# Two extra full-height products behind every first attention pass of the first unit of heads

## What is computed

```
x = x + attention_a(layernorm(x))       # 16 heads of 8, rotary, no mask            "stage a"
x = x + local_stack(layernorm(x))       # 6 layers, windows of 32, feed-forward     "stage b"
x = x + attention_c(layernorm(x))       # 16 heads of 8, rotary, causal mask        "stage c"
x = x + attention_and_experts(x)        # 4 heads, 8 experts                        "stage d"

# attention_a, attention_c, per head:
scores = q @ k.T / sqrt(8)              # attention_c: only keys up to the query
out = softmax(scores) @ v
```

## Time and profile before

| | |
|---|---|
| time, median of 3 runs | 5325.54 us (5321.98, 5325.54, 5348.38) |
| span of the profiled execution, first to last instruction | 5311.3 us |
| lowest run above that span | 10.7 us |
| TensorE matmul (PE) busy | 4908.3 us, 92% |
| TensorE weight load (PEld) busy | 2986.5 us, 56% |
| VectorE (DVE) busy | 4424.3 us, 83% |
| ScalarE (ACT) busy | 3628.7 us, 68% |
| GpSimd (POOL) busy | 2893.4 us, 54% |
| mean granted TensorE clock | 0.959 of 2.4 GHz |

### The profile page before, as it was taken

The page is one execution under the profiler, slowest core; times in us unless marked ns, Lnnn a source line. Parts: engine busy times, 40 slices in busy tenths (PEclk is TensorE's granted clock), DMA queues, the critical chain, the costliest instruction groups (busy, mean ns, idle before and its releaser), DMA issues. The chain is left out here.

```text
span 5311.3 us, 143059 instructions
## 1 busy us (share of the span) xinstructions
PE 4908.3 (92%) x59480; PEld 2986.5 (56%) x59480; DVE 4424.3 (83%) x9261; ACT 3628.7 (68%) x6488; POOL 2893.4 (54%) x3441
## 2 busy tenths in 40 slices
PE   6999997999999999999999999999997999968978
PEld 2333333666666666666666666666664555544445
DVE  7998995989999899999899889999985777677665
ACT  2888885777777777777777777777772777745622
POOL 2121003878777777787778777877761111024634
PEclk6999998999999999999999999999996999988989
DMA  0000101000000000000000000000000000000000
GB/s 23 1 1 1 32 5 39 10 10 14 26 10 10 14 26 10 10 17 26 10 10 14 26 10 10 14 10 10 8 4 25 2 2 2 2 15 1 1 1 17
DMA packets 51737, 63.29 MB, mean 12 GB/s; under 512 B 12820, under 2 KB 41258, under 8 KB 50322
## 3 DMA queue, kind: packets, MB, share of 16 engines
q1 hardware_dynamic: 51090, 54.14, 3.4%
HBM read 25.17 MB, written 4.19 MB: 6 GB/s over the span
## 5 line engine op out<-in xcount | busy, mean ns | idle before, releaser
L1488 POOL TENSOR_TENSOR x<-x,b_norm 128x512 f32<-128x512 f32 x768 | 784.5, 1042 | 350.9 <-DVE b_norm L1353 350.8
L1143 PE MATMUL psum<-b_w_vo,b_mixed 128*128 128x128 f32 x6144 | 830.2, 278 | 2.9 <-ACT b_mixed L1242 1.5
L1143 PEld LDWEIGHTS psum<-b_w_vo,b_mixed 128*128 128x128 f32 x6144 | 753.4, 192 | 68.0 <-issue 51.1
L652 DVE TENSOR_REDUCE a_top<-psum 128x1 f32<-128x512 f32 x1024 | 637.5, 682 | 77.9 <-PE psum L471 75.5
L1479 POOL TENSOR_TENSOR x<-x,b_cross 128x256 f32<-128x256 f32 x768 | 559.6, 729 | 186.4 <-DVE b_cross L1337 185.5
L583 ACT ACTIVATE a_prob<-psum 128x512 f32<-128x512 f32 x1024 | 557.1, 606 | 117.9 <-PE psum L487 108.5
L1212 ACT ACTIVATE b_square<-psum 128x512 f32<-128x512 f32 x768 | 465.5, 606 | 162.8 <-DVE b_norm L1345 144.3
L1345 DVE TENSOR_REDUCE b_norm<-b_square 128x8 f32<-128x512 f32 x768 | 514.1, 673 | 61.3 <-ACT b_square L1212 60.8
L1242 ACT COPY b_mixed<-psum 128x512 f32<-128x512 f32 x768 | 409.1, 588 | 223.4 <-PE psum L1128 223.4
L1481 POOL TENSOR_TENSOR x<-x,b_cross 128x256 f32<-128x256 f32 x768 | 559.5, 728 | 0.0
L1333 DVE TENSOR_TENSOR x<-psum,b_table 128x512 f32<-128x512 f32 x768 | 520.5, 678 | 23.1 <-ACT b_square L1212 23.1
(11 more groups left out here) (321 smaller groups left out, 10471.6 us busy)
## 6 DMA issues: line engine op xcount, KB each, us to landing
b_prev<-b_xs_x SPq DMA_DIRECT2D x24, 384.0 KB, 3.5
b_shifted_x<-y SPq DMA_DIRECT2D x24, 224.0 KB, 2.6
b_shifted_f<-y SPq DMA_DIRECT2D x48, 112.0 KB, 2.1
ab<-in_L_ffn_Wqkv SPq DMA_DIRECT2D x3, 1024.0 KB, 7.0
ab<-in_L_ffn_Wqkv SPq DMA_DIRECT2D x6, 512.0 KB, 7.2
ab<-in_L_ffn_Wo SPq DMA_DIRECT2D x6, 512.0 KB, 8.7
b_w_qk<-in_L_ffn_Wqkv SPq DMA_DIRECT2D x3, 1024.0 KB, 7.2
b_prev<-b_xs_x SPq DMA_DIRECT2D x24, 112.0 KB, 3.4
```

The lines of the kernel that those rows point to most:

```text
L652: e.tensor_reduce(top2[i % 2][:, t, c, head:head + 1], banks[n][:, 0:wide], AX.X, ALU.max).then_inc(emptied[n], 1)
L1143: made = e.matmul(banks[n][:, 0:D], mixed[:, h, :], w_vo[l % 2][:, h, :], start=h == 0, stop=h == 2 * PAIRS - 1)
L1488: e.tensor_tensor(rh, rh, bcast(norm[i % 2][:, 1, HPC * c:HPC * (c + 1)], 2, LDIM), ALU.mult).then_inc(sem["scaled"], 1)
```

## The change

In the branch of TensorE's stream that writes a first pass, two more matmuls follow it when the unit is the stage's first (`i == 0`). They multiply all 128 rows of the same query and key columns (so all four heads at once, full height and width of the array), as wide as the pass itself, into bank 7. Bank 7 holds nothing at that time: the values of unit 0 come later and start it anew, so what these products write is never read. They carry no semaphore. `mha_stage` is built for stage a and for stage c, so both have them: 2 x 64 products in a, 2 x 48 in c.

```diff
@@ -471,6 +471,10 @@
                     e.matmul(banks[n][:, 0:wide], q1[i % 2][part, P * t:P * (t + 1)], kt[i % 3][part, BANK * c:hi],
                              start=not corner, stop=True, skip_group_check=corner,
                              tile_position=(ROWS * head, 0)).then_inc(filled[n], 1)
+                    if i == 0:
+                        for _ in range(2):
+                            e.matmul(banks[7][:, 0:wide], q1[0][:, P * t:P * (t + 1)], kt[0][:, BANK * c:hi],
+                                     start=True, stop=True, skip_group_check=True)
                 if kind == "second":
                     c, k, g = step[2:]
                     lo = max(0, k * P - c * BANK) if causal else 0
```

## The result

The changed kernel takes 5415.6 us as the median of 4 runs (5388.63 to 5420.94), the kernel before 5323.76 us (4 runs, 5313.28 to 5348.38). The ratio is 1.0161, with a 95% interval of 1.0144 to 1.0178: 1.6% slower. The profiled execution spans 5415.3 us and took 5416.56 us, so only 1.3 us lie around a span.

What follows compares the result with a forecast made beforehand. VectorE was taken to bound stage a's start until 72.3 us, then TensorE at 1.2 GHz; with pairs, TensorE throughout. +13 - 4 + 42 = +51 us on 5325.5 gave 5376.5 us; own range 5365 to 5400, whole range 5341 to 5440.

Steps and rivals of the forecast that it cites:

- B: Rival: the clock falls in stage a too, say at VectorE's norms, and stays down; +66 there, 5439 us; chance 0.10.
- D: Rival: the added products take twice the columns or more; at twice, about 5435 us; chance 0.04.
- The bound: Unit 0 of stage a: with the pairs TensorE becomes the bound all through, as VectorE needs only 0.61 us a pass.
- The price of a pass and its pair: First pass plus two products on TensorE: 1.02 us at full clock, 1.76 at half, changes of height included.
- The upper bound given beside it: Price of a pair if each product took 1,024 columns: 1.28 us more at half clock, half that at full.
- E: Rival: changes of height cost next to nothing, only columns count; sum +9, 5335 us; chance 0.03.
- Which clock? At 46 us it is full: Stage a, unit 0: clock full on entry and kept with the pairs; 71.1 us against 58.2, +13.
- Unit 1 of stage a: Entered at full clock instead of half: first 19 passes take 13.3 us in place of 17.0, -4; then the clock falls.
- Stage c: Unit 0: narrow pairs lose the clock, 84.3 us against 37.3, +47, less 5 for the opening: +42; unit 1: 0.
- C: Rival: in stage c the clock returns after the transposes for about half; 42 shrinks to about 22, 5355 us; chance 0.19.
- Rival A: Clock holds at 1.00 through unit 0 and the start of unit 1 in both stages; +7, 5332 us; chance 0.11.
- The time around the span: Whole kernel: the span of 5311.3 us lies 10.7 below the lowest of three runs, 14.2 below their median.

Runs made afterwards that it cites:

- the entry filled: Changed kernel plus dense float32 products ahead of unit 0: 21 (stage c 15) before turn_k, 3 before turn_q1, gaps closed; 5391.74 us, ratio 1.0138.
- The control: Kernel before plus the same dense float32 products ahead of unit 0, without pairs behind the passes; 5320.96 us, ratio 1.0005.

## Why the prediction was right, and where not

The direction and the range held (5341 to 5440), but 5415.6 us lie outside the forecast's own 5365 to 5400: the loss was 92 us where 51 were forecast. The range held it because it was drawn wide enough for B and D.

- **The bound.** Right. TensorE is the bound in both units 0, without a gap, and VectorE waits for it.
- **The price of a pass and its pair.** Right in kind, a little low. 1.76 us at half clock were forecast, 1.87 measured; 1.02 and 1.09 at full. The pass's 0.72 was exact; the pair took 1.15 in place of 1.04, four transposes being a good but not perfect stand-in. An fp32r product goes through once: a pair takes 1.15 us at half clock, and twice the columns alone would be 1.71, so D falls. (The upper bound given beside it is miscounted: 1,024 columns a product add 0.85 us a pair at half clock, not 1.28. D itself has the right sum.) E falls too: one product in place of two left 75 of 92 us, and seven tenths of the loss in the units 0, where columns alone would leave half.
- **The failed step: "Which clock? At 46 us it is full".** I took the clock on entry from one execution of the kernel before, where nothing in unit 0 depended much on it. With the pairs it decides: in stage a they kept the clock that they found, for 72 us at full and 92 at half. In the profiled execution it was half, and stage a cost +52.7 in place of +9. With the entry filled it cost 12.6, within the forecast's ends of +5 and +13, and in five of ten executions with stage a alone the whole loss was 3 to 10 us. The term was right where its condition held, which by the two groups is about every other time. This was rival B but for its ways: B had the clock fall at a norm and stay down (+66), while it never was up at the entry and came back at 138.9 us, behind transposes and a projection between pairs. With the condition met the sum is still low: 69 us with the entry filled, in place of 51.
- **Unit 1 of stage a.** Right: 19 passes in 11.9 us at full clock where 13.3 were forecast, and the clock fell again before the values, for 17.0 us.
- **Stage c.** The mechanism was right, the size low: +42 forecast, +50.5 in unit 0 of the profiled execution, +52 with stage c alone. Unit 0 took 87.8 us against the 84.3 worked out, the pair's price again; the 5 us taken off for a clock that comes back had no ground, it stayed at 0.50 to the end. C didn't happen.
- **Rival A and the rule behind it.** No. TensorE was busy 84.40 of 84.40 us in stage c at a clock of 0.50, and the 3.4 us before, at 1.00, had no gap either. The Trainium skill ("TensorE: Matmul & The Clock Gate", section Why this matters for your kernels) asks for no idle gaps; here that was not enough. The row that the prediction set against A doesn't show this: the clock fell at 48.7 us, and in the 3.4 us before, at 1.00, TensorE was busy only 2.13 us, which left idle time as a cause. The products of 32 rows show it (busy 3.35 of 3.40 us, then 0.50), and stage c of the changed kernel does. In these traces the full clock lasted longest where full-height products of 512 columns stood behind the passes; narrow pairs, products of 32 rows and bare passes lost it. Which property of the work decides isn't shown.
- **The time around the span** was taken as 10.7 us and is 1.3; the other 9 are the spread between executions. It didn't enter the sum, which was put on the median.

What stays open: of the 70.7 us between the spans of the filled entry and of the kernel before, about 13 are in stage a and about 47 in the start of stage c, counted by the starts of VectorE's same instructions in both. About 4 lie between the two stages and about 6 around the end of stage c. There the clock stood at 0.50 for 27.3 us in a row (4662.5 to 4689.8), in the kernel before for 6.8 (4605.5 to 4612.3). The control, entry without pairs, has the same 27.3 us (4595.4 to 4622.7), so it comes without the pairs too. The clock falls and rises there at other places in each execution, and no run says why.

## What to carry to other kernels

A filler that is to keep TensorE's clock has to be priced at both clocks, and the clock at its entry belongs to the price: at full clock this one would have cost 5 to 13 us in stage a, at half clock it cost 50. Put fillers behind groups of row-tiled steps, not behind each: a change of height has a price each time (one product in place of two left four fifths of the loss, some of it by the clock), and the same 224 products cost 92 us one pair at a time and nothing on balance in groups of four, where the clock was higher too. When a term rests on a state that one execution shows, look at how the executions spread before taking it: two groups of times in one kernel, with two mean clocks, say more than the median between them.

## What the runs showed of the hardware that was not expected

- The same work held either clock: the same pass and pair, back to back, ran 92 us at 0.50 in the changed kernel and 72 us at 1.00 with the entry filled.
- The same transposes, with a wait of 0.5 us among them, brought the clock up at 45.3 us in the profiled execution of the kernel before and not in that of the changed kernel, nor in that with stage c's pairs alone. The instructions ahead of them are the same; their times aren't quite, for the projections took 7.67 us in the first and 8.31 in the second. What decides isn't shown.
- With stage a's pairs alone, ten executions of one program fell into 5323 to 5330 and 5363 to 5390 us.
- In groups of four the products cost nothing on balance: 5323.2 us with all 224 of them, 5322.9 without, at mean clocks of 0.961 to 0.968 against 0.951 to 0.958.
